# New order of scan pairs, folded MLP norm and later token loads in a Mamba, expert and attention kernel

## The chip, the cores and the metric

One core of one Trainium2 chip. The metric is the device time of the kernel in microseconds, the median of three runs. Five engines work side by side and meet at semaphores only: TensorE (PE), VectorE (DVE), ScalarE (ACT), GpSimd (POOL) and SyncE (SP), which issues the DMAs.

## What is computed

Four layers, each added to its input after a layer norm, on `x` of shape (4, 1024, 256): a selective scan, a mixture of 8 experts of which each token takes 2, a causal linear attention with an MLP, and the same experts once more.

```python
# scan (32 states per channel, 1024 steps in order)
s = jnp.clip(s * A + b_t[:, None, :] * x_t[:, :, None], -10.0, 10.0)
y = jnp.sum(c_t[:, None, :] * s, axis=-1)
...
# experts
h = jnp.maximum(jnp.einsum('nd,edh->neh', xf, w1) + b1, 0.0)
eo = jnp.einsum('neh,ehd->ned', h, w2) + b2
out = jnp.einsum('ne,ned->nd', comb, eo)
...
# attention layer, second half
y = layer_norm(x, ln2_scale, ln2_bias)
y = jax.nn.gelu(y @ w1 + b1) @ w2 + b2
return x + y
```

## The kernel before

`front_part` makes the operands of the scan (normed input, projections, convolution) for the whole sequence and leaves them in DRAM; it ends at about 155 us. `main_part` cuts the sequence into 16 chunks of 64 time steps (of 4 batches: 256 tokens, two tiles of 128). Each engine runs a program of its own, written out by hand as `step(i, c, late)` and turned 14 times in a loop, with single steps ahead and behind. One step holds three chunks at three stages: the scan of chunk `i`; output projection, first experts and attention of chunk `c = i - 1`; MLP and second experts of chunk `late = i - 2`. I call one such step a pass.

The scan is serial. Two time steps are a pair, 32 pairs to a chunk. For pair n, PE makes the inputs (`scan_inputs`, L972, products of B and x rows), DVE makes the new states: in `scan_pair`, each of two steps and two halves has a product with the decay (L1389) and a sum with limits (L1399). Every second pair PE reads the states out (`scan_output`, L988). In PE's program `scan(1)` issues the input of pair n + 1 and, at even n from 2 on, the output of the two pairs before; the input of pair n + 1 waits (`stepped`) until DVE has done pair n - 1. In DVE's program `scan(1)` does pair n. Where `scan` stands in the two programs is the order of the work: pairs lie between the pieces of the other two chunks, to fill gaps on both engines.

The other pieces, on PE: `first_layer` (L1054, three products of high and low parts) and `second_layer` (L1067) of an expert, with the suffix `late_` for the late chunk; `gate` (L1024), `turn_comb` (L1031, transposes the tokens' weights for the experts), `bias` (L1038), transposes (`tpose_set`, L1009), `features`, `scores` (L1148), `from_states` (L1158), `from_chunk` (L1168), `new_states` (L1179), `mlp_input`, `mlp_first`, `mlp_second`. The output projection of attention is L1332. On DVE: `ln_stats`, `ln_apply` (L1428, subtract and scale), `ln_affine` (L1435 and L1440, the same with weight and bias, two instructions a tile for one), `routing` (L1447 to L1459, picks two of eight), `set_acc` (L1475), `add_expert` (L1486), `feature`, `mask` (L1503). ACT copies, and makes relu and gelu between the layers. POOL makes the reciprocal roots of the norms (L799, L801), the low parts (L808) and some additions (L822, L838, L842).

At the start of the main part ACT makes high parts of `f_w1` and `m_w1` (L862) and POOL their low parts, while DVE begins the scan.

SP's `chunk_loads` asks for the tokens of chunk `i` (12 DMAs, L720 to L722) and then for x rows (8 DMAs per four units, L704) and B rows (4 DMAs per unit, L713); a unit is two pairs. Rows are asked for four units ahead, as soon as PE has made the inputs of the unit whose place they take. Ahead of the tokens SP waits in `tokens_free` until the chunk before has used its own:

```python
with looped(sp, 2, CHUNKS - 1) as i:
    tokens_free(i - 1)
    chunk_loads(i, True)
    finish(i - 2)
```

## Time and profile before

| | |
|---|---|
| median of 3 runs | 2336.93 us (2328.58 to 2338.21) |
| profiled execution, its own time | 2337.66 us |
| its span, first to last instruction | 2335.9 us |
| PE busy | 2029.0 us, 87% |
| DVE busy | 1696.1 us, 73% |
| ACT busy | 517.3 us, 22% |
| POOL busy | 259.5 us, 11% |
| mean granted clock of TensorE | 0.923 |

Busy is the time in which an engine runs an instruction; waits for semaphores are not in it. The granted clock is the share of 2.4 GHz that TensorE was given; it knows two levels, 1.0 and 0.5 (1.2 GHz). A row `A <- B: x, n, y` of the view of waits says that A's engine sat idle x us in n times, the longest y, until B had ended. PE instructions of the source appear as two in the trace where they are full float32 products (L1067: 4 in the program, 8 in the trace). The scan runs from 170.7 to 2175.7 us, the first chunk alone, and behind the last there are two more steps without scan.

### The profile page before, as it was taken

Reading aid. Unit: us, or ns where it says so; the run is one execution under the profiler, and the core shown is the slowest. Engines: PE = TensorE matmul, PEld = TensorE weight load, DVE = VectorE, ACT = ScalarE, POOL = GpSimd, SP = SyncE. Lnnn points to the kernel's source line nnn. Section 1 sums busy time; section 2 is a strip of 40 time slices with the busy share of each in tenths; the row PEclk is TensorE's granted clock in tenths of the full one; section 3 lists DMA queues with packets and bytes.
Section 4 is the critical chain, followed back from the end, with each engine's and each line's share of the span. In section 5 each row is a group of like instructions: output and inputs, shape, how many; then the busy total and the mean of one; then the engine's idle time right before and its main releaser. Section 6 shows DMA issues by size and latency. Waiting matters only on the chain. (4 is left out here: it accounts for less than half of the span.)

```text
span 2335.9 us, 58987 instructions
## 1 busy us (share of the span) xinstructions
PE 2029.0 (87%) x18400; PEld 1656.8 (71%) x18400; DVE 1696.1 (73%) x6417; ACT 517.3 (22%) x1078; POOL 259.5 (11%) x337
## 2 busy tenths in 40 slices
PE   7845888989898989989898989889898989899897
PEld 4422666768777777777787778778687777778786
DVE  4539768787787878787876877786786868787542
ACT  3430112121222222121222222221212222221221
POOL 0021001010101110010101111110101011010110
PEclk9875779999999999999998999998998989999998
DMA  7731100000000101010100001010000001010000
GB/s 254 229 109 34 25 12 25 12 25 12 23 18 12 28 9 30 12 30 12 25 12 17 24 12 25 12 30 12 25 12 23 18 12 25 12 30 8 6 1 10
DMA packets 100872, 73.51 MB, mean 31 GB/s; under 512 B 64488, under 2 KB 94448, under 8 KB 99568
## 3 DMA queue, kind: packets, MB, share of 16 engines
q1 hardware_dynamic: 100592, 69.91, 10.7%
q8 instruction: 160, 2.62, 0.5%
q14 instruction: 120, 0.98, 0.1%
HBM read 46.26 MB, written 23.59 MB: 30 GB/s over the span
## 5 line engine op out<-in xcount | busy, mean ns | idle before, releaser
L1389 DVE TENSOR_TENSOR decayed_state<-state,decay 128x128 f32<-128x128 f32 x2048 | 552.0, 311 | 9.9 <-issue 8.0
L1399 DVE CUSTOM_DVE_ANT_0 state<-decayed_state,bank 128x128 f32<-128x128 f32 x2048 | 504.7, 286 | 46.5 <-PE bank L972 19.1
L1067 PE MATMUL bank<-f_w_sb,hs_whole 128*128 128x256 f32 x2048 | 526.2, 402 | 0.6 <-ACT hs_whole L877 0.6
L1067 PEld LDWEIGHTS bank<-f_w_sb,hs_whole 128*128 128x128 f32 x2048 | 390.2, 200 | 87.6 <-ACT hs_whole L877 31.2
L877 ACT ACTIVATE hs_whole<-bank,f_b_sb 128x256 f32<-128x256 f32 x512 | 215.1, 471 | 947.4 <-PE bank L1054 947.4
L972 PE MATMUL bank<-xrows,brows 128*128 128x256 f32 x1024 | 258.2, 345 | 94.9 <-DVE state L1399 56.0
L972 PEld LDWEIGHTS bank<-xrows,brows 128*128 128x128 f32 x1024 | 179.7, 211 | 140.5 <-issue 74.4
L1486 DVE SCALAR_TENSOR_TENSOR x<-bank,comb,x 128x256 f32<-128x256 f32 x256 | 111.9, 478 | 147.9 <-PE bank L1067 147.3
L1486 DVE SCALAR_TENSOR_TENSOR res<-bank,comb,res 128x256 f32<-128x256 f32 x256 | 112.1, 480 | 138.2 <-PE bank L1067 136.6
L988 PE MATMUL bank<-state,cblk 128*32 128x256 f32 x2048 | 178.3, 423 | 35.0 <-DVE state L1399 35.0
L799 POOL TENSOR_TENSOR m_ve<-m_mv,m_eps 128x2 f32<-128x2 f32 x96 | 19.3, 201 | 1580.1 <-DVE m_mv L1423 1580.1
L1054 PE MATMUL bank<-late_fT_parts,f_w_hi 128*128 128x256 f32 x1024 | 187.3, 307 | 0.0
L1054 PE MATMUL bank<-fT_parts,f_w_hi 128*128 128x256 f32 x1024 | 172.9, 294 | 0.0
L1054 PEld LDWEIGHTS bank<-late_fT_parts,f_w_hi 128*128 128x128 f32 x1024 | 149.3, 195 | 12.1 <-issue 6.4
L1054 PEld LDWEIGHTS bank<-fT_parts,f_w_hi 128*128 128x128 f32 x1024 | 141.6, 193 | 6.7 <-issue 5.3
L1067 PE MATMUL bank<-m_w_sb,hs_whole 128*128 128x256 f32 x512 | 120.7, 379 | 0.0
L893 ACT ACTIVATE hs_whole<-bank,m_b_sb 128x256 f32<-128x256 f32 x128 | 53.8, 471 | 225.4 <-PE bank L1054 225.4
L1067 PEld LDWEIGHTS bank<-m_w_sb,hs_whole 128*128 128x128 f32 x512 | 92.4, 189 | 10.1
L988 PEld LDWEIGHTS bank<-state,cblk 128*32 128x32 f32 x2048 | 42.0, 113 | 74.5 <-DVE state L1399 39.3
L1054 PE MATMUL bank<-late_fT_parts,m_w_hi 128*128 128x256 f32 x512 | 90.7, 301 | 2.0 <-issue 2.0
L1054 PEld LDWEIGHTS bank<-late_fT_parts,m_w_hi 128*128 128x128 f32 x512 | 74.0, 199 | 17.5 <-issue 16.3
L1054 PE MATMUL bank<-late_fT_parts,f_w_lo 128*128 128x256 f32 x512 | 83.4, 286 | 0.0
(148 smaller groups left out, 2561.5 us busy)
## 6 DMA issues: line engine op xcount, KB each, us to landing
xrows<-xs_dram SPq DMA_DIRECT2D x512, 32.0 KB
brows<-bs_dram SPq DMA_DIRECT2D x1024, 2.0 KB
xt<-in_x SPq DMA_DIRECT2D x4, 1024.0 KB, 7.9
xn_dram<-xn SPq DMA_DIRECT2D x4, 1024.0 KB, 5.4
z_dram<-zT SPq DMA_DIRECT2D x4, 1024.0 KB, 4.1
f_w_sb<-in_f_w SPq DMA_DIRECT2D x2, 2048.0 KB
xs_dram<-xhi SPq DMA_DIRECT2D x4, 1024.0 KB, 5.2
xs_dram<-xlo SPq DMA_DIRECT2D x4, 1024.0 KB, 8.4
```

Of the source, the lines that this page charges most:

```text
L799: pool.tensor_tensor(ve[:, k], mv[:, k, :, 1], eps[:, k], ALU.add).then_inc(ve_done[k].sem, 1)
L877: act.activation(hs_whole[:, e % 2, m], hidden_bank(c, f, e)[:, m * TOK:(m + 1) * TOK], ACT.Relu, bias=g["f_b1"][:, e, m:m + 1]).then_inc( ...
L893: act.activation(hs_whole[:, j % 2, m], HB[j % 2][:, m * TOK:(m + 1) * TOK], ACT.Gelu_apprx_tanh, bias=g["m_b1"][:, 2 * j + m:2 * j + m + ...
L972: last = pe.matmul(U[n % 2][:, j * D:(j + 1) * D], brows[:, q * USTEPS + tq].rearrange("r b n -> r (b n)"), xrows[:, half % 2, tq, :], sta ...
L988: last = pe.matmul(Y[YCOLS * j:YCOLS * (j + 1), tile * D:(tile + 1) * D], cblk[:, slot * YCOLS:(slot + 1) * YCOLS], state[:, s % RING, :], ...
L1054: last = pe.matmul(dst(tile), *((w_, d_) if stationary == "w" else (d_, w_)), start=first and stationary != "more", stop=(n == len(PRODUCT ...
L1067: last = pe.matmul(bank_[:, tile * D:(tile + 1) * D], hs_whole[:, slot, m, tile * P:(tile + 1) * P], w(m), start=(m == 0 and tile == 0 and ...
L1389: dve.tensor_tensor(decayed_state[:, part], state[:, (s - 1) % RING, part], decay[:, part], ALU.mult).then_inc(decayed.sem, 1)
L1399: dve._custom_dve(add_sat, out=state[:, s % RING, part], in0=decayed_state[:, part], in1=U[n % 2][:, s % 2 * D + h * HALF:s % 2 * D + (h + ...
L1486: dve.scalar_tensor_tensor(out=dst[:, tile], in0=out_bank(c, f, e)[:, tile * D:(tile + 1) * D], scalar=comb[:, f, tile, e:e + 1], in1=dst[ ...
```

## The change

**Scan pairs.** Both programs get new places for `scan`. In the loop over the first experts a table `PAIRS_AT` gives the number of pairs ahead of each expert: none at 0, two at 1, 6 and 7, one at the others. Ahead of the loop stands one pair less, and some places in attention lose their pair, others move. **Order on PE.** `second_layer(c, 0, 0)` goes ahead of `turn_comb`, with a wait for `x3_done`, since the accumulator bank of expert 0 still holds the MLP output. `late_second(5)` goes ahead of `from_states`, `late_first(6)` ahead of `from_chunk(1)`. On DVE the norm for the late experts and the four masks are drawn together.

**Folded norm.** The norm ahead of the MLP loses weight and bias (`ln_apply` for `ln_affine`). At the start, ACT scales the rows of `m_w1` with `ln2_s`, PE multiplies `ln2_b` with the unscaled `m_w1`, and DVE adds that to `m_b1`. The high and low parts are made behind it.

**Tokens.** SP asks for the tokens of a chunk behind the rows of its first five units, `tokens_free` with them.

```diff
-            def chunk_loads(i, more):
-                load_tokens(sp, i)
+            def chunk_loads(i, more, earlier=True):
                 for u in range(UNITS_U if more else UNITS_U - GROUPS_U):
+                    if u == TOKENS_AT:
+                        if earlier:
+                            tokens_free(i - 1)
+                        load_tokens(sp, i)
...
+            act.wait_ge(mlp_bias_made.sem, 1)
+            for k in range(KD):
+                act.activation(g["m_w1"][:, k, :], g["m_w1"][:, k, :], ACT.Copy, scale=g["ln2_s"][:, k:k + 1]).then_inc(mlp_scaled.sem, 1)
+            act.wait_ge(mlp_scaled.sem, KD)
+            act.wait_ge(mlp_bias_set.sem, 1)
...
+            for m in range(MLP // P):
+                for k in range(KD):
+                    last = pe.matmul(TB[:, 2 * m:2 * m + 2], g["m_w1"][:, k, m * P:(m + 1) * P],
+                                     g["ln2_b"][:, k:k + 1].broadcast_to([P, 2]), start=(k == 0), stop=(k == KD - 1))
+            last.then_inc(mlp_bias_made.sem, 1)
...
+        PAIRS_AT = (0, 2, 1, 1, 1, 1, 2, 2)
...
                     tpose_set(c, T_FFN1, xf_done[0])
-                scan(1)
                 mlp_second(3)
                 scan(1)
...
                     first_layer(c, 0, 1)
-                scan(2)
+                scan(1)
+                if c is not None:
+                    if late is not None:
+                        pe.wait_ge(x3_done.sem, x3_done.after(late, 1))
+                    second_layer(c, 0, 0)
+                scan(1)
                 if c is not None:
                     turn_comb(c, 0)
...
                         if e:
-                            scan(1)
+                            scan(PAIRS_AT[e])
...
-                        second_layer(c, 0, e)
+                        if e:
+                            second_layer(c, 0, e)
                         if e == 0:
                             bias(c, 0)
-                            scan(1)
...
                 late_first(3)
-                scan(1)
                 late_second(2)
...
                 features(g["wk"], 0, k_made)
-                scan(1)
...
                 pe.wait_ge(kT_done.sem, kT_done.after(c, 1))
+                scan(1)
                 features(g["wq"], 0, q_made)
...
                 scan(1)
+                late_second(5)
                 pe.wait_ge(masked.sem, masked.after(c, 3))
...
                 from_chunk(0)
-                late_second(5)
-                scan(1)
+                scan(1)
+                late_first(6)
                 from_chunk(1).then_inc(num_made.sem, 1)
                 new_states(0).then_inc(kv_half.sem, 1)
-                late_first(6)
                 scan(1)
...
                 tpose_set(c, T_WO, at_done, HB[1])
-                scan(1)
                 late_second(6)
```

And DVE's program:

```diff
-                scan(3)
+                scan(1)
                 if late is not None:
...
                     ln_stats(late, FFN2, x3, x3_done, (1, 1))
+                scan(1)
                 if c is not None:
                     routing(c, 0)
-                scan(2)
+                scan(1)
+                if late is not None:
+                    ln_apply(late, FFN2, x3, late_turn, xf_done[1])
                 if c is not None:
                     set_acc(c, 0, res, res)
                 for e in range(E):
                     if e:
-                        scan(1)
+                        scan(PAIRS_AT[e])
...
-                ln_affine(LN2, a_t, "ln2_s", lambda tile: rows["ln2_b"][:], late_turn, yl_done)
+                ln_apply(c, LN2, a_t, late_turn, yl_done)
```

The pair between late additions 1 and 2, that between masks 1 and 2 and that ahead of late addition 6 are gone from DVE; one goes behind the key features and one behind late addition 5. The pairs left over come behind the last late addition, three on PE before and four now.

Three places of PE's program in the loop's body show the moves. The listings carry the line numbers of their own kernel: L972, L988, L1031, L1038, L1054 and L1067 of the one are L990, L1006, L1049, L1056, L1072 and L1085 of the other. `REGISTER_ALU` and `ISA` hold waits and counters.

Entry to the first experts, behind the first layers of experts 0 and 1, before:

```order
L972 MATMUL bank<-xrows,brows 128x256 x2
L969 REGISTER_ALU
L972 MATMUL bank<-xrows,brows 128x256 x2
L982 REGISTER_ALU
L988 MATMUL bank<-state,cblk 32x256 x4
L1031 MATMUL bank<-ident_sb,comb 8x128 x2
L1085 ISA
L1067 MATMUL bank<-f_w_sb,hs_whole 128x256 x4
L1038 MATMUL bank<-f_b_sb,combT 128x256 x2
L969 REGISTER_ALU
L972 MATMUL bank<-xrows,brows 128x256 x2
```

The same place now:

```order
L990 MATMUL bank<-xrows,brows 128x256 x2
L1006 MATMUL bank<-state,cblk 32x256 x4
L1103 ISA
L1085 MATMUL bank<-f_w_sb,hs_whole 128x256 x4
L987 REGISTER_ALU
L990 MATMUL bank<-xrows,brows 128x256 x2
L1049 MATMUL bank<-ident_sb,comb 8x128 x2
L1056 MATMUL bank<-f_b_sb,combT 128x256 x2
```

The second layer has moved ahead of the transposes of `comb`, and the bias product follows these at once.

From the second layer of expert 6 to the first late first layer, before:

```order
L1067 MATMUL bank<-f_w_sb,hs_whole 128x256 x4
L969 REGISTER_ALU
L972 MATMUL bank<-xrows,brows 128x256 x2
L982 REGISTER_ALU
L988 MATMUL bank<-state,cblk 32x256 x4
L1054 MATMUL bank<-late_fT_parts,f_w_hi 128x256 x4
```

and now:

```order
L1085 MATMUL bank<-f_w_sb,hs_whole 128x256 x4
L987 REGISTER_ALU
L990 MATMUL bank<-xrows,brows 128x256 x2
L1000 REGISTER_ALU
L1006 MATMUL bank<-state,cblk 32x256 x4
L982 REGISTER_ALU
L984 REGISTER_ALU
L987 REGISTER_ALU
L990 MATMUL bank<-xrows,brows 128x256 x2
L1072 MATMUL bank<-late_fT_parts,f_w_hi 128x256 x4
```

A second input stands directly behind the first.

Ahead of `from_states` (the 64x68 products), behind late first layer 5, before:

```order
L972 MATMUL bank<-xrows,brows 128x256 x2
L988 MATMUL bank<-state,cblk 32x256 x4
L1313 REGISTER_ALU
L1314 REGISTER_ALU
L1158 MATMUL bank<-kv,qT 64x68 x16
L1168 MATMUL bank<-vv,ss 64x17 x32
L1085 REGISTER_ALU
L1067 MATMUL bank<-f_w_sb,hs_whole 128x256 x4
```

and now:

```order
L990 MATMUL bank<-xrows,brows 128x256 x2
L1006 MATMUL bank<-state,cblk 32x256 x4
L1143 REGISTER_ALU
L1103 REGISTER_ALU
L1085 MATMUL bank<-f_w_sb,hs_whole 128x256 x4
L1335 REGISTER_ALU
L1176 MATMUL bank<-kv,qT 64x68 x16
L1186 MATMUL bank<-vv,ss 64x17 x32
```

Late second layer 5 has moved from behind the first `from_chunk` to ahead of `from_states`.

## Rows read from the trace of the kernel before

**Rows 1.** Windows, three passes: length; PE, PEld, DVE, ACT, POOL busy; PEclk; DMA.
```profile
1135.93:1269.30 133.37, 121.58 (x1127) 102.44 (x1127) 100.32 (x390) 28.55 (x61) 14.46 (x19) 0.92 0.07 17
1269.30:1396.21 126.91, 114.38 (x1126) 96.20 (x1125) 100.30 (x390) 28.53 (x61) 14.45 (x19) 0.97 0.08 19
1396.21:1524.98 128.77, 115.19 (x1125) 96.74 (x1124) 100.83 (x390) 28.54 (x61) 14.48 (x19) 0.97 0.08 20
```

**Rows 2.** Who PE waited for, 365 to 2178 us; last line: 2178 to 2336.
```profile
PE bank L1009 <- DVE late_turn L1440: 50.0, 14, 3.6
PE bank L988 <- DVE state L1399: 30.4, 14, 3.0
PE bank L1158 <- DVE ss L1503: 23.5, 14, 1.7
PE bank L972 <- DVE state L1399: 20.3, 14, 1.5
PE bank L1031 <- DVE comb L1459: 18.0, 14, 1.3
PE bank L972 <- DMA brows<-bs_dram: 16.4, 13, 1.5
PE bank L1148 <- ACT ktok L886: 8.8, 14, 0.6
...
PE bank L1038 <- ACT combT L882: 0.5, 1, 0.5
```

**Rows 3.** Three short stretches (columns as in rows 1; PEclk is the granted clock).
```profile
1233.00:1247.00 14.00, 14.00 (x196) 12.23 (x194) 3.69 (x15) 0.84 (x2) 0.00 (x0) 0.51 0.02 4
1366.00:1380.00 14.00, 14.00 (x292) 12.59 (x289) 7.57 (x28) 1.44 (x3) 0.00 (x0) 1.00 0.03 6
1424.00:1428.00 4.00, 4.00 (x24) 2.88 (x24) 2.44 (x11) 0.84 (x2) 0.00 (x0) 0.57 0.03 6
```

**Rows 4.** Timeline around the last experts: start, us, engine, line, operation.
```profile
1322.02 0.58 PE L972 MATMUL bank<-xrows,brows 128*128 128x256 f32 x2
1322.54 0.64 PE L988 MATMUL bank<-state,cblk 128*32 128x256 f32 x8
1323.11 0.74 PE L1054 MATMUL bank<-late_fT_parts,f_w_hi 128*128 128x256 f32 x4
...
1324.61 1.89 PE L1067 MATMUL bank<-f_w_sb,hs_whole 128*128 128x256 f32 x8
...
1322.50 0.88 DVE L1486 SCALAR_TENSOR_TENSOR res<-bank,comb,res 128x256 f32<-128x256 f32 x2 [1.21 <-PE bank L1067]
```

**Rows 5.** Timeline around the MLP norm, DVE and POOL.
```profile
1380.96 0.49 DVE L1389 TENSOR_TENSOR decayed_state<-state,decay 128x128 f32<-128x128 f32 x2
...
1382.08 1.34 POOL L842 TENSOR_TENSOR mb<-mb,a_t 128x512 f32<-128x512 f32 x1
...
1382.63 1.46 DVE L1435 SCALAR_TENSOR_TENSOR late_turn<-a_t,m_mv,ln_s_sb 128x256 f32<-128x256 f32 x2
...
1384.02 0.87 DVE L1440 SCALAR_TENSOR_TENSOR late_turn<-late_turn,m_rstd,ln_b_sb 128x256 f32<-128x256 f32 x2
```

**Rows 6.** Timeline of SP, the first of 12 token loads and what follows the last.
```profile
375.95 0.56 SPq L720 DMA_DIRECT2D x_t<-in_x  x1
...
384.47 3.27 SPq L704 DMA_DIRECT2D xrows<-xs_dram  x8
```

**Rows 7.** Timeline at the start of the main part.
```profile
166.88 1.89 ACT L862 ACTIVATE m_w_hi<-m_w_sb 128x2048 fp32r<-128x2048 f32 x1
167.15 8.83 POOL L808 TENSOR_TENSOR f_w_lo<-f_w_sb,f_w_hi 128x4096 fp32r<-128x4096 f32 x1 [4.52 <-ACT f_w_hi L862]
...
170.74 0.49 DVE L1399 CUSTOM_DVE_ANT_0 state<-decayed_state,bank 128x128 f32<-128x128 f32 x2 [5.90 <-PE bank L972]
171.15 9.48 DVE L1389 TENSOR_TENSOR decayed_state<-state,decay 128x128 f32<-128x128 f32 x2
175.93 4.55 POOL L808 TENSOR_TENSOR m_w_lo<-m_w_sb,m_w_hi 128x2048 fp32r<-128x2048 f32 x1
```

More of the change, by code:

```diff
@@ L118, in build @@
         feature_eps = weight("feature_eps", [P, 1])
-        back = [("a_log", a_log), ("own_batch", own_batch), ("out_w", out_w), *rows.items(),
+        back = [("a_log", a_log), ("own_batch", own_batch), ("out_w", out_w), *rows.items(), ("ln2_s", ln2_s), ("ln2_b", ln2_b),
                 ("gate_w", gate_w), ("gate_b", gate_b), ("before", before), ("f_w1", f_w1), ("f_b1", f_b1),
@@ L1570, in step @@
                 add_late(1)
-                scan(1)
                 add_late(2)
@@ L1586, in step @@
                 mask(1, False)
-                scan(1)
                 mask(2, False)
@@ L1591, in step @@
                 add_late(5)
+                scan(1)
                 dve.wait_ge(num_made.sem, num_made.after(c, 1))
```

27 lines of the change are left out of this document (15 added, 12 removed).

## The prediction, made before the changed kernel was run

> **What bounds the kernel now.** I read four views, in this order. First the span cut into passes. In the steady part a pass is one turn of the loop `step(i, i - 1, i - 2)`, 14 of them between 365.5 and 2178.0 us. They come in three lengths [rows 1]: five of about 127 us, five of about 129 and four of about 133.3; the row shown for each length stands for the others. PE (TensorE) is busy for some 115 us of a 127 us pass, DVE (VectorE) for 100. So PE is the engine to fill, and DVE, with 27 us to spare, matters where PE waits for it.
>
> Second, who PE waits for, over the same 14 passes [rows 2]. The seven rows add up to 167.4 us, 11.96 a pass: 3.57 before the transposes of the MLP input (L1009), 2.17 before scan outputs, nearly all at the end of a pass, 1.68 before `from_states` (L1158), 1.45 before one scan input (L972), 1.29 before the transposes of the expert weights of the tokens (L1031), 1.17 before a scan input whose B rows had not landed, 0.63 before `scores` (L1148). Nearly all of them are PE waiting for DVE, so it is the order of the two programs that costs, not their amount of work.
>
> Third, the granted clock [rows 3]. After `from_states` one pass has level 0.51 (1.2 GHz) over 14 us, and another has 1.00 (2.4 GHz) at the same place: that is the 133 us pass against the 127 us one, 6.4 us. Before the fall PE had sat 1.67 us for the masks and then run the small products. Even the shortest pass has 0.97 [rows 1], so it falls somewhere in each. The 129 us passes differ from the 127 ones by a short fall about 28 us into the pass (0.57 over 4 us, third row of rows 3), behind the L1031 wait, the bias and the wait for rows: 1.9 us each. Over the shortest pass the four long ones cost 25.6 us and the five middle ones 9.5, together 35.
>
> Fourth, the timeline, for unit prices [rows 4, 5]. A scan input takes 0.5 us of PE behind a second layer and 0.3 elsewhere, an output 0.6, a first layer 1.5. On DVE one expert's addition takes 0.8 to 0.9 (0.88 with its end), and a pair of scan steps 1.67 (1380.96 to 1382.63). PE can do the input of pair n+1 only when DVE has done pair n-1, and this ties the two.
>
> **The change, part by part, for one full pass.**
>
> *Token loads behind five units.* SP issued 12 loads of tokens ahead of the rows (375.95 to 384.47, 8.5 us [rows 6]). Now the rows for pair 8 are asked for as soon as pair 1 has its inputs. The wait of 1.17 goes to 0. What is late next: the rows of the tenth unit, now behind the tokens. They are asked for after pair 10, and needed by pair 18, in between lie some 30 us of expert work against about 15 us of issues. I charge nothing.
>
> *Second layer of expert 0 ahead of the transposes.* Its 1.7 us of PE work cover the routing on DVE; 1.29 goes to 0. But now the bias product comes directly behind the transposes and needs ScalarE's copy. The last pass has the two back to back already, and there the wait is 0.5 (the last line of [rows 2]). Net -0.8.
>
> *Two pairs at expert 1, none at 0.* At pair 7 PE needs pair 6 from DVE, which stands behind the accumulator (about 0.8, like an addition) and expert 0: 0.1 + 0.8 + 0.8 + 1.67 = 3.4 us after the bias. PE has a first layer and pair 6 for this time, 1.5 + 0.9. New wait 1.0.
>
> *Two pairs at experts 6 and 7.* At 6 the same sum with the late bias leaves 0.3. At 7, PE's pair 15 needs pair 14, which DVE begins only after adding expert 6: 0.1 + 0.8 + 1.67 = 2.55 after the second layer, while PE has pair 14 alone, 0.85. New wait 1.7. Formerly the late first layer stood behind a single pair here, and no wait.
>
> *Pairs taken from the first half of attention.* Between the late layers 3 and 2 no pair stands any more, and the input after the attention transposes finds its pair done long ago: 1.45 goes to 0. `scores` keeps 0.5 of 0.63, as it still needs late expert 4 and the K copy.
>
> *Late second layer 5 ahead of `from_states`.* 1.7 us of PE work lie over the last two masks: 1.68 goes to 0.1. ScalarE's relu is ready in time, since a pair stands between the two layers. DVE's wait for `num_made` grows, but there it has room.
>
> *Folded MLP norm.* DVE's two products that apply the bias (1384.02 to 1384.89) go: 0.9. Pair 27, which is now last ahead of the transposes, has no output, so PE arrives 0.6 sooner. 3.57 becomes 3.2. The other two products took 1.46 instead of about 0.9 because GpSimd's addition (1382.08, 1.34 us) ran beside them [rows 5], and I let the new `tensor_scalar` suffer the same 0.6; ends 0 and 1.3. The Trainium skill, "SBUF — State Buffer", section "Who interferes with whom", says that such a DVE instruction, if GpSimd came first, is blocked fully until the other ends. By that rule it would end about 0.2 later, and the sum would be 3 us longer.
>
> *One more pair behind the MLP input* (four, were three). From the end of late second layer 7: 0.1 + 0.8 + three pairs (5.0) + 0.1 = 6.0 until the last output may start; PE has 3.5 of work there. 2.17 becomes 2.5.
>
> Sum of waits after: 0.5 + 1.0 + 0.3 + 1.7 + 0 + 0.5 + 0.1 + 3.2 + 2.5 = 9.8, against 11.96: **-2.1 a pass, -29 us over 14.** Each of the three new waits could be nothing, if DVE runs ahead, or one pair (1.67) longer, so a pass lies between -5 and +1.
>
> *The clock.* The long falls came behind 1.67 us of wait and then the small products. The wait goes, but 3 us of small products stay, and `from_chunk(1)`, both calls of `new_states` and the transposes now stand together. The new 1.0 and 1.7 us waits are as large as those behind which the short falls came. I take a quarter of the 35 back: **-8**; ends -35 and +35.
>
> *Start.* 16 small products of `ln2_b` with `m_w1` come ahead of the first scan input, which comes so late that DVE waits 5.9 us for it [rows 7]: hidden. But ScalarE scales `m_w1` (as many elements as take it 1.89 us [rows 7]) and waits for those products first, about 6 us in all, before it makes the high parts. GpSimd's two low parts (8.83 and 4.55 us) move by as much, and it is their end that frees DVE: two scan products took 9.48 us beside them [rows 7]. DVE gets one pair (1.7) done before they begin. The stall of the fifth unit's rows in the first chunk (about 2.8 us) goes, and one of about 2 comes behind the tokens, as SP is full there. **+4**, between 0 and +7.
>
> *First pass with a late chunk missing* (242.8 to 365.5): the same moves at a lower clock, with 29 us of PE waits: -1, between -4 and +3. *The last two passes*: no scan, the fold and the masks: **-1**.
>
> Total: -29 - 8 + 4 - 1 - 1 = -35. The profiled execution took 2337.7 us (its span 2335.9), the median of the runs is 2336.9, so either base gives the same: **2303 us**.
>
> **Rivals.** What separates change from no change in a measurement of this kernel is about 0.5%, 12 us.
>
> *A: the clock gains more than the waits.* If filling the waits keeps the level up in all passes, all 35 us come back: 2303 - 27 = 2276. For it: both kinds of falls lay directly behind waits that go. Against: new waits of the same size. "TensorE: Matmul & The Clock Gate", section "Loop structure matters more than you think", of the Trainium skill, says that matmuls kept back to back stay at the high clock and that waits between them lose it; by that rule this rival holds, if one overlooks the new waits.
>
> *B: the double pairs take it all.* If each of the three doubled places, and the tail, costs PE half to one pair more than I worked out, 2.1 a pass comes back and the time is about 2332. For it: scan steps in a row are DVE's longest work, and PE has only an input between them. Against: the sums above.
>
> *C: slower, by falls of the clock.* If the denser block of small products behind late first layer 6, or the wait of 1.7 at expert 7, brings the 14 us fall in nearly every pass instead of four, ten more passes cost 6.4 each: 2311 + 64 = 2375. It decides from about six more passes on. For it: PE stayed at the low level through just these products [rows 3]. Against: after them now come late second layer 6, the output projection and late first layer 7, which are dense, so that the level should rise sooner.
>
> *D: tokens in the way.* If the rows behind the tokens land late in each pass, 1.2 to 2 us come back per pass: 2320 to 2331. The issues take half of the time that there is, so this is unlikely.
>
> **How the numbers follow.** Forecast 0.46 (2288 to 2325), A 0.22, B 0.15, C 0.10, D 0.07. Faster by over 0.5% are the forecast, A, and a part of B and D: 0.75. Within 0.5% the rest of B and D: 0.15. Slower C: 0.10. The range goes down to the clock gain in full with 1 us a pass more (2265) and up through B to no change (2338).
>
> **What would show it.** Right: no PE wait at L1158, none for B rows in the full passes; waits of PE near 9.8 a pass, with new ones of about 1 and 1.7 among the scan inputs of the expert loop; the MLP wait near 3.2; the first scan step of chunk 1 about 4 us later. Wrong: waits over 12 a pass (B), or more than four passes at granted clock 0.92 or below (C), or none (A).

## The result and the profile after

| | before | changed |
|---|---|---|
| median of 18 runs each, in turns | 2327.34 us (2319.49 to 2345.17) | 2354.76 us (2336.19 to 2363.58) |
| profiled execution, its own time | 2337.66 us | 2353.65 us |
| its span | 2335.9 us | 2351.8 us |
| PE, DVE busy | 2029.0, 1696.1 us | 2049.6, 1688.1 us |
| mean granted clock | 0.923 | 0.918 |

The ratio is 1.0104, with a 95% interval of 1.0082 to 1.0127: slower by 1.0%, 27 us. The forecast was 2303. It started from 2337, the median of three runs; over 18 runs the kernel before has 2327, and the profiled execution of before is 10 us above that, so the two traces lie closer together (15.9 us) than the two medians.

I cut the span at the first scan step of chunks 0, 1 and 2, at the end of the last scan step, and at the end. The two profiled spans differ by 15.9 us: start of the scan +2.8 (170.74 to 173.55), chunk 0 +4.8, chunk 1 -4.6, the 14 full passes +11.2 (1810.0 to 1821.2), tail +1.7. So most of the loss is in the passes, where I had forecast a gain of 37. Three of them, with the columns of [rows 1], and short stretches behind expert 7 in two of them:

```profile
1017.56:1150.73 133.17, 118.84 (x1125) 99.11 (x1124) 100.11 (x388) 28.37 (x61) 14.42 (x19) 0.94 0.08 20
1282.47:1413.20 130.73, 116.63 (x1125) 97.78 (x1124) 99.61 (x388) 28.38 (x61) 14.36 (x19) 0.96 0.08 21
1805.67:1932.90 127.23, 116.20 (x1126) 97.45 (x1125) 99.58 (x389) 28.30 (x61) 14.37 (x19) 0.96 0.08 19
1073.00:1078.00 5.00, 4.70 (x21) 4.22 (x22) 2.06 (x11) 0.84 (x2) 0.00 (x0) 0.66 0.03 5
1338.00:1342.00 4.00, 3.56 (x23) 3.36 (x24) 2.20 (x11) 0.84 (x2) 0.00 (x0) 1.00 0.03 6
```

The shortest pass is 126.8 us, as long as the shortest of before, the longest 133.5. Who PE waited for, 368.5 to 2189.8 us (to be laid beside [rows 2]):

```profile
PE bank L990 <- DVE state L1422: 67.7, 42, 2.7
PE bank L1027 <- DVE late_turn L1451: 54.8, 14, 3.9
PE bank L1072 <- issue: 12.4, 12, 1.5
PE bank L990 <- issue: 12.0, 5, 3.1
PE bank L1166 <- ACT ktok L899: 8.9, 14, 0.7
PE bank L1056 <- ACT combT L895: 6.5, 14, 0.5
PE bank L1006 <- DVE state L1422: 0.7, 1, 0.7
PE bank L1219 <- DVE z_t L1537: 0.5, 1, 0.5
```

The waits for DVE's masks (L1158 of before), its weights of the tokens (L1031) and the B rows are gone, as forecast. In the passes PE waited 163.5 us in all, 10.5 less than before (174.0, with short ones that [rows 2] leaves out), not 29. Two things eat the rest: 24.4 us called "issue", for which before has 3.5, and the MLP wait, which went up from 50.0 to 54.8 where it should have gone down by 5. One of the "issue" waits, PE at the head of a pass (start, us, operation, and in brackets the idle time before it):

```profile
1282.27 0.63 PE L1072 MATMUL bank<-late_fT_parts,m_w_hi 128*128 128x256 f32 x4
1282.74 0.39 PE L1072 MATMUL bank<-late_fT_parts,m_w_lo 128*128 128x256 f32 x2
1284.60 0.51 PE L1072 MATMUL bank<-late_fT_parts,m_w_lo 128*128 128x256 f32 x2 [1.47 <-issue]
```

It stands in the middle of a product of one layer; nothing that PE could wait for in data lies there. The profile's list of DMA queues has a hint. Instructions come to the core through queues of their own; first the row of before, then that of the changed kernel (packets, MB, share):

```profile
q8 instruction: 160, 2.62, 0.5%
```

```profile
q8 instruction: 172, 2.82, 0.5%
```

These packets have 16 KB. Sorted by time, before has ten in nearly every pass, the changed kernel eleven. The trace shows some 2,370 instructions of PE in a pass, 237 for each of ten packets. I take the queue to be PE's; the runs with a shift, below, bear that out.

And the clock: 197 us of the passes ran at half clock, 167 before. It fell at about 57 us of a pass in nine of the fourteen passes, where before it never did: that is the stretch 1073 to 1078 above, behind expert 7. The wait there stands in every pass, so in five of them it had no fall behind it; 1338 to 1342 is one of these.

### The profile page after: what moved, and what is told of

The parts are those of the page before. It is cut to its first block and busy times, and to the rows that moved or that the text cites. A ratio compares the mean times of both kernels' runs of the same rounds, so it can differ in the third digit from the quotient of the medians.

```text
span 2351.8 us, 59011 instructions
## 1 busy us (share of the span) xinstructions
PE 2049.6 (87%) x18432; PEld 1669.7 (71%) x18432; DVE 1688.1 (72%) x6386; ACT 518.1 (22%) x1080; POOL 258.3 (11%) x337
## 5 line engine op out<-in xcount | busy, mean ns | idle before, releaser
L1412 DVE TENSOR_TENSOR decayed_state<-state,decay 128x128 f32<-128x128 f32 x2048 | 565.1, 317 | 10.4 <-issue 7.8
L1085 PE MATMUL bank<-f_w_sb,hs_whole 128*128 128x256 f32 x2048 | 529.7, 404 | 3.4 <-DVE ss L1526 1.0
L1085 PEld LDWEIGHTS bank<-f_w_sb,hs_whole 128*128 128x128 f32 x2048 | 394.0, 202 | 95.0 <-ACT hs_whole L890 37.8
L990 PE MATMUL bank<-xrows,brows 128*128 128x256 f32 x1024 | 258.8, 342 | 126.0 <-DVE state L1422 107.0
L990 PEld LDWEIGHTS bank<-xrows,brows 128*128 128x128 f32 x1024 | 174.6, 205 | 195.1 <-DVE state L1422 121.5
L1509 DVE SCALAR_TENSOR_TENSOR res<-bank,comb,res 128x256 f32<-128x256 f32 x256 | 112.1, 479 | 126.5 <-PE bank L1085 125.1
L1006 PE MATMUL bank<-state,cblk 128*32 128x256 f32 x2048 | 183.9, 433 | 3.3 <-DVE state L1422 2.4
L1072 PE MATMUL bank<-late_fT_parts,f_w_hi 128*128 128x256 f32 x1024 | 184.3, 304 | 0.0
L1072 PE MATMUL bank<-fT_parts,f_w_hi 128*128 128x256 f32 x1024 | 172.6, 294 | 0.0
L1072 PEld LDWEIGHTS bank<-late_fT_parts,f_w_hi 128*128 128x128 f32 x1024 | 149.4, 195 | 6.0 <-issue 0.7
L1072 PEld LDWEIGHTS bank<-fT_parts,f_w_hi 128*128 128x128 f32 x1024 | 139.5, 191 | 11.6 <-issue 10.3
L1085 PE MATMUL bank<-m_w_sb,hs_whole 128*128 128x256 f32 x512 | 121.7, 381 | 0.0
L1072 PE MATMUL bank<-late_fT_parts,m_w_hi 128*128 128x256 f32 x512 | 101.9, 329 | 0.0
L1085 PEld LDWEIGHTS bank<-m_w_sb,hs_whole 128*128 128x128 f32 x512 | 93.3, 192 | 10.3
L1072 PEld LDWEIGHTS bank<-late_fT_parts,m_w_hi 128*128 128x128 f32 x512 | 84.2, 225 | 15.4 <-issue 14.4
L1027 PE MATMUL bank<-ident_sb,late_turn 128*128 128x128 f32 x128 | 25.0, 330 | 66.7 <-DVE late_turn L1451 66.7
L1072 PE MATMUL bank<-late_fT_parts,f_w_lo 128*128 128x256 f32 x512 | 83.0, 285 | 0.0
```

Source lines behind the costliest of these rows:

```text
L990: last = pe.matmul(U[n % 2][:, j * D:(j + 1) * D], brows[:, q * USTEPS + tq].rearrange("r b n -> r (b n)"), xrows[:, half % 2, tq, :], sta ...
L1006: last = pe.matmul(Y[YCOLS * j:YCOLS * (j + 1), tile * D:(tile + 1) * D], cblk[:, slot * YCOLS:(slot + 1) * YCOLS], state[:, s % RING, :], ...
L1027: last = pe.transpose(dst[:, kk * TOK + tile * P:kk * TOK + (tile + 1) * P], src[:, tile, kk * P:(kk + 1) * P], ident[:])
L1072: last = pe.matmul(dst(tile), *((w_, d_) if stationary == "w" else (d_, w_)), start=first and stationary != "more", stop=(n == len(PRODUCT ...
L1085: last = pe.matmul(bank_[:, tile * D:(tile + 1) * D], hs_whole[:, slot, m, tile * P:(tile + 1) * P], w(m), start=(m == 0 and tile == 0 and ...
L1412: dve.tensor_tensor(decayed_state[:, part], state[:, (s - 1) % RING, part], decay[:, part], ALU.mult).then_inc(decayed.sem, 1)
```

## The experiments

All but one were measured in five rounds (the exception in three), in turns with the kernel before. I give for each run: the 14 passes in its profiled execution, PE's waits in them, the passes less the waits ("work"), and the part at half clock, summed from the trace's record of the granted clock. A profiled execution is one run; the median is of 5 to 18. The four rows of repeats are the same built programs once more (see below) and show how far two executions of one program lie apart: 12 us in the passes and 24 us at half clock between before and e4, 17 at half clock between e1 and e12.

| run | passes | waits | work | half clock | median | ratio, 95% |
|---|---|---|---|---|---|---|
| before | 1810.0 | 174.0 | 1636.0 | 167 | 2327 to 2330 | |
| changed | 1821.2 | 163.5 | 1657.7 | 197 | 2354.76 | 1.0082 to 1.0127 |
| repeat of before (e4) | 1798.4 | 174.7 | 1623.7 | 143 | 2328.96 | 0.9984 to 1.0033 |
| repeat of changed (e6) | 1813.9 | 159.9 | 1654.0 | 187 | 2352.14 | 1.0061 to 1.0156 |
| e1 fold | 1813.9 | 180.9 | 1633.0 | 159 | 2345.71 | 1.0026 to 1.0091 |
| repeat of e1 (e5) | 1809.4 | 178.7 | 1630.7 | 150 | 2342.13 | 1.0033 to 1.0088 |
| repeat of e1 (e12) | 1807.2 | 181.0 | 1626.2 | 142 | 2344.77 | 1.0039 to 1.0091 |
| e2 tokens | 1766.9 | 161.7 | 1605.2 | 95 | 2294.88 | 0.9827 to 0.9901 |
| e3 order | 1812.7 | 168.2 | 1644.5 | 182 | 2347.55 | 1.0061 to 1.0139 |
| e8 tokens, order | 1811.5 | 167.4 | 1644.1 | 171 | 2347.99 | 1.0062 to 1.0114 |
| e7 tokens, fold | 1820.4 | 175.5 | 1644.9 | 200 | 2355.56 | 1.0073 to 1.0143 |
| e13 before, shifted 64 | 1831.1 | 194.0 | 1637.1 | 171 | 2360.70 | 1.0116 to 1.0227 |
| e14 fold, shifted 192 more | 1776.7 | 163.9 | 1612.8 | 113 | 2316.14 | 0.9936 to 0.9988 |
| e15 tokens, fold, 192 | 1767.9 | 148.4 | 1619.5 | 125 | 2318.21 | 0.9928 to 1.0006 |
| e16 changed, 192 | 1790.5 | 153.2 | 1637.3 | 142 | 2343.20 | 1.0046 to 1.0108 |
| e9 both parts of the order | 1797.0 | 161.4 | 1635.6 | 143 | 2338.47 | 1.0022 to 1.0068 |
| e10 expert part | 1772.1 | 158.1 | 1614.0 | 106 | 2304.05 | 0.9868 to 0.9924 |
| e11 tokens, layer 5 early | 1767.2 | 138.0 | 1629.2 | 146 | 2299.20 | 0.9860 to 0.9916 |
| e17 e10 and attention's pairs | 1787.6 | 152.1 | 1635.5 | 164 | 2319.76 | 0.9933 to 0.9981 |
| e18 e10 and attention's layers | 1753.7 | 142.5 | 1611.2 | 81 | 2293.79 | 0.9817 to 0.9886 |

Two readings of the table carry the rest. The work is the same products in every row and yet runs from 1605 to 1658 us; it goes up with the time at half clock, by some 0.4 us for each (30.8 us from e2 to before, at 72 us more of half clock). That is rough: e16, with the new order, and e4 have the same half clock and 13.6 us between their work, and this part was not explained. And the passes are waits plus work: who takes waits away can lose them again as clock.

**The three parts alone.** e1 has the fold alone, all `scan` calls as before. e2 has the tokens alone. e3 has the new places of pairs and layers alone, on both engines, with `ln_affine` as before.

```diff
-                load_tokens(sp, i)
                 for u in range(UNITS_U if more else UNITS_U - GROUPS_U):
+                    if u == TOKENS_AT:
+                        if earlier:
+                            tokens_free(i - 1)
+                        load_tokens(sp, i)
```

> The kernel before with the folded norm alone, old order and old token loads. Theory 1, code placement: the 16 products at the start stand ahead of PE's loop and shift its code; the changed kernel shows waits of PE for no releaser ('issue') of 1.2 us two microseconds into a pass and of 3 us at its head, 24.4 us over 14 passes, which before had 3.5. If the shift makes them, this kernel shows them too: start +6 us (PE's products took 7.0 us where I had 6 and hidden), passes -0.9 each by the shorter chain (-13) and +20 by the waits, together +10 to +18. Theory 2, the order alone is to blame: no such waits here, start +6, chain -13: -12 to -2.

> The kernel before with the token loads behind five units alone. Both theories: the wait for B rows (16.4 us over the full passes) goes, the first chunk is about the same: -10 to -20 us. If the rows were late for another reason: 0. If the freed 1.2 us a pass are given back by the scan input behind them (DVE's state): -3 to 0.

> The kernel before with the new order of both programs alone (scan pairs, second layers, DVE's norm and masks), old norm, old token loads. Theory 2, the new waits of 1.0 and 1.9 us in the expert loop and the falls of the clock behind them (56 to 57 us into the pass in ten passes of the changed kernel) cost more than the removed waits gave: +10 to +25 us. Theory 1: the order gives what it should, -5 to -20 us, if the loop keeps its place; PE's program ahead of the loop has the same length here but for a few waits.

Measured: fold 2345.71, tokens 2294.88, order 2347.55. Only the smallest edit is fast, and it is faster than both kernels. The fold came out as theory 1 had it, the order as theory 2; the tokens gained twice what I expected. e2's waits fell by 12 us, its work by 31 (by 13 and 18 against e4). Before, the clock fell behind the wait for rows in five passes, 28 us into them; here are the same places of a pass in the trace of before and in that of e2, and then the place 97 us into a pass where before had its long falls and one whole pass of e2:

```profile
522.50:527.50 5.00, 5.00 (x29) 3.71 (x28) 2.34 (x11) 0.84 (x2) 0.00 (x0) 0.66 0.03 6
```

```profile
521.00:526.00 5.00, 5.00 (x40) 4.20 (x39) 4.48 (x18) 1.93 (x4) 0.07 (x1) 1.00 0.19 52
1476.00:1490.00 14.00, 12.91 (x263) 11.06 (x261) 9.92 (x39) 3.24 (x8) 1.35 (x3) 1.00 0.02 3
1503.98:1630.27 126.29, 114.44 (x1126) 96.96 (x1126) 100.93 (x390) 28.54 (x61) 14.47 (x19) 0.97 0.08 19
```

Both kinds of falls are gone, in all 14 passes; thirteen of the passes have 126.2 to 126.5 us. The order alone also removes the wait for rows (16.4 to 1.2 us), and those for masks and for the tokens' weights. But its waits in all go down by 6 us only, since the MLP wait grew from 50.0 to 67.9 and two new places stand among the scan inputs, and it has its own falls: half clock 182 us, 151 of them from 108 us of the pass on, where before has 97.

```profile
PE bank L973 <- DVE state L1402: 72.9, 41, 2.8
PE bank L1010 <- DVE late_turn L1443: 67.9, 14, 4.9
```

e3 has 160 packets on q8, as before, and 2 us of "issue": its loss has nothing to do with them. The fold alone takes 14 us off the MLP wait and gets 12.9 of "issue" at the head of the pass in return.

**Empty instructions that were none.** The bias products are 64 more instructions for PE ahead of its loop. I wanted to test whether their place is what matters, with `pe.nop(nofuse=True)` ahead of the main part: 64 in before (e4), 192 in the fold, the changed kernel and tokens with fold (e5, e6, e7), 32 in the fold (e12).

> The kernel before with 64 empty instructions on PE ahead of the main part's first product, where PE waits for rows anyway; nothing else. It shifts the loop's code by what the 16 products take (32 products and 32 weight loads in the trace). Theory 1: waits of PE for no releaser near the head of the pass, as in the changed kernel, and +12 to +25 us. Theory 2: no difference, within 0.3%.

> The kernel before with the folded norm alone, and 192 empty TensorE instructions ahead of the main part. With the bias products' 64 instructions they move TensorE's loop by 256 instructions, as much as one of the 16 KB packets that reach the core ten times in a pass of before and eleven times in a pass of the folded one. Theory (code placement): the folded norm alone lost because its loop then spans an eleventh packet, and TensorE waits for it some 1.4 us a pass (17.8 us counted as issue, at rows of the pass where before has 3). Then this run has ten packets a pass, under 5 us of issue waits and keeps the norm's gain of 1.0 us a pass: 2310 to 2325 us, ratio 0.992 to 0.998. Rival (the fold itself, by the clock's falls or the start): the waits stay, and the time stays at 2340 to 2350, ratio 1.003 to 1.009.

> The changed kernel with the same 192 empty TensorE instructions. Theory (code placement): ten packets a pass instead of eleven, the 24 us of issue waits fall under 5, and the time falls from 2354 by 15 to 25 us, to 2330 to 2340, ratio 1.000 to 1.005. Rival (placement doesn't matter): 2348 to 2360, ratio above 1.008. In either case the clock's falls behind expert 7 stay, so that half clock time in the fourteen passes stays over 170 us.

> Tokens behind five units of rows and the folded norm, no new order, with the 192 empty instructions. If parts add up and placement was the fold's loss: the tokens' 34 us less and the norm's 10 to 15 us less, 2278 to 2290 us, ratio 0.978 to 0.984, with the MLP wait near 2.7 us a pass and no wait for rows. If the fold itself costs: 2300 to 2315. If the tokens' gain was a clock state that any other timing loses: 2315 to 2335.

> Tokens behind five units and the new order, no folded norm (so the full change without the fold). The order alone had lost the wait for rows already, so by the theory that the order's loss is its own (wait at expert 7 and fewer pairs in the attention part, clock falling behind both) the tokens add little here: 2340 to 2352 us, ratio 1.005 to 1.010, half clock time 170 to 190 us. If parts add up instead, the tokens' 34 us come off 2347: 2310 to 2320, ratio 0.992 to 0.996, and the changed kernel's loss would lie with the fold.

> The kernel before with the folded norm and 32 empty TensorE instructions. With 192 of them TensorE's packets kept their places in the pass, as they did with 64 in the kernel before; the packets may start at multiples of 64 instructions, so that only the rest of a division by 64 counts. Theory: with 32 the packets move by up to 32 instructions against the program; ten a pass instead of eleven and no issue waits, 2320 to 2335. Rival: eleven packets and the waits stay, 2340 to 2350, as with 192.

Measured: e4 2328.96 (1.0008), e5 2342.13 (1.0061), e6 2352.14 (1.0108), e12 2344.77 (1.0065). These are the numbers of before, e1 and the changed kernel once more, and for a plain reason: the built programs hold none of the empty instructions (q8 has 160 packets in e4, as in before, and 172 or 173 in the others). So they say nothing on placement, for or against either theory, but they show how well the ratios repeat: the fold has 1.0059, 1.0061, 1.0065. e7 is tokens with fold: 2355.56, and the tokens' 34 us are gone; I had 2278 to 2335 in three cases, and none of them holds. Its loop has the fold's place, with 27.8 us of "issue" and 200 us at half clock. e8 is the order with tokens: 2347.99 against 2347.55 without. The order had freed the wait for rows already, and the tokens bring nothing more, as I had expected (2340 to 2352). Put the other way round, the order on top of the tokens costs 53 us (e2 to e8); of the 45 us by which the passes differ, 39 are work. The parts do not add up.

**Placement, with instructions that stay.** Waits that are already met stay in the program (two in the source make one). They stand where PE idles ahead of the main part, 128 in the source and 64 in the program for e13, 384 and 192 for e14, e15 and e16:

```diff
+            for _ in range(128):
+                pe.wait_ge(pool_set.sem, 1)
             pe.wait_ge(g["back_in"], BACK_IN)
```

> The kernel before with 64 waits that are already met at the head of TensorE's main part, where it idles 17 us: its loop then lies 64 instructions further on, as the folded norm's bias products place it, and nothing else is changed. (The empty instructions of the runs labelled pad had been dropped when those kernels were built, so that they were repeats: of before, of the fold, of the changed kernel and of tokens with fold.) Theory (code placement): eleven 16 KB packets a pass instead of ten, 13 to 25 us of issue waits at the head of the passes, time up by 8 to 20 us: 2336 to 2348, ratio 1.003 to 1.008. Rival (placement does nothing; the waits come from the fold): ten packets, 2325 to 2332.

> The kernel before with the folded norm and 192 waits already met, so that TensorE's loop lies 256 instructions further on than before. Theory: ten packets a pass, issue waits under 5 us, 2310 to 2325 us, ratio 0.992 to 0.999. Rival: eleven packets and 2340 to 2348 again.

> Tokens behind five units and the folded norm, with the 192 waits already met. Without them it took 2356 us, with 28 us of issue waits and 155 us at half clock in the passes. Theory (placement took the fold's gain and set off the clock's falls): ten packets, no issue waits, half clock near the 64 us of the tokens alone, and the norm's 1.0 us a pass: 2278 to 2292 us, ratio 0.979 to 0.985. Rival (the fold itself sets off the falls, by another phase): 2300 to 2345.

> The changed kernel with the 192 waits already met. Theory: ten packets, the 24 us of issue waits gone, the order's own loss left (tokens with the order took 2348), less the norm's gain: 2325 to 2340, ratio 0.999 to 1.005. Rival (placement doesn't matter): 2350 to 2360.

e13 took 2360.70 us: the kernel before, with nothing changed but the place of its loop, is 1.7% slower. Its packets and PE's waits over the passes, against [rows 2]:

```profile
q8 instruction: 172, 2.82, 0.5%
```

```profile
PE bank L1011 <- DVE late_turn L1442: 50.3, 14, 3.6
PE bank L990 <- DVE state L1401: 29.6, 13, 3.1
PE bank L974 <- DMA brows<-bs_dram: 24.6, 13, 2.1
PE bank L1160 <- DVE ss L1505: 23.5, 14, 1.7
...
PE bank L1056 <- issue: 13.6, 13, 1.8
```

The second instruction queue, q14, keeps its 120 packets. The time is above the theory's range (2336 to 2348), the packets and the waits are the theory's. The waits for DVE are as before to 1 us; added are 13.6 us in the MLP's products at the head of the pass, and 8 us at the rows, 20 in all. Start and tail are as before (170.0 and 160.7 us): what is added lies in the passes. Against the profiled execution of before it is 21 us, nearly all of them waits; against e4, whose time is nearer to the median, it is 33 us, 19 of them waits and 13 work, at 28 us more of half clock. And the other way round, e14 (fold, shifted by 64 + 192 = 256 instructions against before, about one packet by the count above) has its ten packets and its waits back:

```profile
q8 instruction: 161, 2.64, 0.5%
```

```profile
PE bank L1006 <- DVE state L1420: 36.6, 13, 2.9
PE bank L1027 <- DVE late_turn L1449: 36.0, 14, 2.6
PE bank L1176 <- DVE ss L1524: 22.1, 14, 1.6
...
PE bank L990 <- issue: 3.6, 13, 0.3
```

Its passes take 37 us less than e1's, its median is 29.6 us lower; the 192 waits cost 11 us at the start (scan from 185.8 us, e1 174.8). So the fold in itself is a gain, and lost by where it put the loop. One control is missing: before with 256 instructions more and no fold was not run. In e16 the changed kernel's passes fall from 1821.2 to 1790.5; the waits called "issue" go from 24.4 to 2.2, of which 12 come back as waits for DVE. Its median falls by 11.6, with 13 us given to the start (186.5 against 173.6), and lies above the 2325 to 2340 of the theory. Without that price it would stand near 2330, level with before; this sum was not run. e15 did not come to 2278 to 2292 as the theory had it. Its passes go up and down in turn:

```profile
1013.08:1141.39 128.31, 116.77 (x1125) 98.62 (x1124) 100.98 (x389) 28.49 (x61) 14.53 (x19) 0.95 0.08 20
1141.39:1265.68 124.29, 114.09 (x1127) 96.47 (x1127) 99.53 (x389) 28.49 (x61) 14.47 (x19) 0.98 0.08 19
```

The shorter kind is 2 us under e2's pass (10.2 us of waits against 11.8); the longer one, with 11.5 us of waits, lies 2 us above it, with a fall at its head and another about 95 us into it. The mean is e2's pass. Its time lies in the rival's range (the clock falls in another phase), and the falls are there: 125 us at half clock against 95. (By the count of the table e2 has 95 us at half clock and e7 has 200, where the expectation has 64 and 155.) Against e7, which is e15 without the 192 waits, it is 37 us faster.

**What in the order loses.** e9: tokens and order, with one pair at expert 7 and the pair between late layers 1 and 2 back. e10: of that order only the expert part. e17 and e18 add to e10 either kind of attention's moves, and e9 has both.

```diff
-        PAIRS_AT = (0, 2, 1, 1, 1, 1, 2, 2)
+        PAIRS_AT = (0, 2, 1, 1, 1, 1, 2, 1)
```

That is in all four. e11 has, on top of e2, this alone (and e18, on top of e10, the same and `late_first(6)` ahead of `from_chunk(1)`):

```diff
                 scan(1)
+                late_second(5)
                 pe.wait_ge(masked.sem, masked.after(c, 3))
...
                 from_chunk(0)
-                late_second(5)
                 scan(1)
```

e17, on top of e10, moves pairs alone (PE's part; DVE's likewise):

```diff
                 features(g["wk"], 0, k_made)
-                scan(1)
...
                 pe.wait_ge(kT_done.sem, kT_done.after(c, 1))
+                scan(1)
...
                 tpose_set(c, T_WO, at_done, HB[1])
-                scan(1)
```

> Tokens behind five units and the new order, but with one pair at expert 7 instead of two, and the pair between the last expert layers 1 and 2 back at its old place. Theory (the double pair at expert 7 costs a wait of 1.9 us, behind which the clock falls at 57 us of a pass): no fall between 50 and 70 us of a pass (tokens and order had 17 us of half clock there, the changed kernel 31), the wait at pair 15 gone, 10 to 20 us less than the 2348 of tokens with the full order: 2328 to 2338. Rival (the loss lies in the attention part, half clock from 108 us of a pass on): 2340 to 2350, and the half clock time there stays at 130 to 150 us.

> Tokens behind five units and the expert part of the new order alone (two pairs at experts 1 and 6, the second layer of expert 0 early), with one pair at expert 7, so that the attention part and the end of the pass are as before. If the order's loss lies in its attention part: near the tokens alone, 2290 to 2305, ratio 0.984 to 0.991, half clock time under 100 us. If it lies in the expert part: 2320 to 2345.

> Tokens behind five units, and the second layer of expert 5 moved ahead of the attention read from the states, where the kernel before waits 1.6 us a pass for the masked scores. Theory (a wait that hides nothing is worth its length, as long as no clock fall is set off): 14 passes less 1.5 us, 2270 to 2280 us, ratio 0.976 to 0.980. Rival (the wait returns at the next operation, since the chain of VectorE sets the pass): 2290 to 2300, the time of the tokens alone. Third: the move sets off falls of the clock as the full order did, 2310 to 2340.

> As e10 (tokens, expert part with one pair at expert 7), and of the attention part the scan pairs' new places alone: the second expert layers 5 and 6 stay where they were. Theory (with the pairs gone from the attention part and more of them at the end of the pass, VectorE's chain of the MLP's norm starts as late as before, and the part around 108 to 124 us, in which TensorE runs the pairs with waits, falls to half clock more often): MLP wait up from 3.6 to 4.5 us or more a pass, half clock in 108 to 124 us of the passes up from 75 to about 115 us, 2325 to 2338 us, ratio 0.999 to 1.004. Rival (the layers' moves cost it): 2300 to 2310.

> As e10, and of the attention part the moves of the last experts' layers alone (second layer of expert 5 ahead of the read from the states, first layer of expert 6 ahead of the second half from the chunk), all scan pairs as in e10. The move of layer 5 alone on top of the tokens took away the 1.6 us wait for the scores in each pass and gave no time, since the clock fell in 13 of 14 passes at 100 to 108 us of the pass. Theory (pairs are the loss): 2300 to 2312 us, ratio 0.988 to 0.993, with such falls. Rival (the layers' moves are the loss): 2325 to 2338.

*The double pair at expert 7.* The changed kernel, around pair 15:

```profile
1205.52 0.88 DVE L1509 SCALAR_TENSOR_TENSOR res<-bank,comb,res 128x256 f32<-128x256 f32 x2 [0.66 <-PE bank L1085]
...
1205.55 0.64 PE L1006 MATMUL bank<-state,cblk 128*32 128x256 f32 x8
...
1208.10 0.50 PE L990 MATMUL bank<-xrows,brows 128*128 128x256 f32 x2 [1.91 <-DVE state L1422]
1208.33 0.54 PEld L1072 LDWEIGHTS bank<-late_fT_parts,f_w_hi 128*128 128x128 f32 x4
```

The addition of expert 6 ends at 1206.4, then come two steps of pair 14; PE waits 1.91 us. This wait is in all 14 passes, and the clock falls right behind it in nine passes of the changed kernel, in five of e8 and four of e3, so the wait by itself does not decide it. In e9, where the wait is gone, there is no fall between 50 and 70 us of any pass; half clock is 171 - 143 = 28 us less than in e8, 17 of them in that stretch, and the median is 9.5 us lower, just above the theory's 2328 to 2338. e9 also puts back the pair between the late layers 1 and 2, and with it a wait of 1.45 us; the two were not tried apart.

*Attention.* e10 (2304.05, 106 us at half clock) has the time that I gave for a loss in the attention part, 9 us over e2. From there the pairs' moves cost 16, the layers' moves gain 10, and both together cost 34. With the pairs gone the MLP wait is 67.9 us instead of 49.9 (e9 and e17 alike), and half clock goes from 106 to 164 us (e17), mostly between 108 and 124 us of the pass. The MLP wait and the half clock are those that e17's theory had, the time (2319.76) lies between its range and the rival's; e18 is under both of its ranges. Neither kind alone explains e9: 29 us come only from the two together.

*Layer 5 alone* (e11) shows how a wait taken away can be worth nothing. Against e2 its waits are 23.7 us lower, as forecast, and its passes are the same to 0.3 us. The time (2299.20) is the rival's, but not for the rival's reason: the wait did not return. What ate it is what the third case has. In all 14 passes the clock falls at about 100 us of the pass, where e2 has no fall:

```profile
1354.00:1358.00 4.00, 4.00 (x83) 2.96 (x84) 1.76 (x9) 0.84 (x2) 0.00 (x0) 0.57 0.00 0
1379.76:1506.02 126.26, 115.91 (x1126) 97.65 (x1126) 100.76 (x391) 28.54 (x61) 14.62 (x19) 0.96 0.08 19
```

PE was busy for the whole of these 4 us, with late first layer 6 above all. For the 6 us before them it was busy too, on small products with one scan input between:

```profile
1347.46 1.17 PE L1159 MATMUL bank<-kv,qT 128*64 128x68 f32 x32
1348.56 2.04 PE L1169 MATMUL bank<-vv,ss 64*64 64x17 f32 x64
1350.53 0.50 PE L973 MATMUL bank<-xrows,brows 128*128 128x256 f32 x2
1350.96 2.04 PE L1169 MATMUL bank<-vv,ss 64*64 64x17 f32 x64
1352.94 0.73 PE L1180 MATMUL bank<-vv,ktok 64*32 64x17 f32 x64
1353.60 0.74 PE L1055 MATMUL bank<-late_fT_parts,f_w_hi 128*128 128x256 f32 x4
```

In e2 late second layer 5 stands in the middle of this block, 2 us of 128x256 products. In e18 layer 5 has moved too, but late first layer 6 stands there in its place, and this fall is there in one pass only. That fits, but nothing was run to test it, and the long falls of before came with layer 5 in the middle. e18 is the fastest kernel of the study: 2293.79 us (2287.09 to 2298.75), 1.5% under before. Against e2 (2294.88) that is no difference that can be told.

## Why the prediction was wrong

**Most waits that I followed by their instructions came out well. Two steps failed: the list of waits had no term for PE's own instructions, and the clock's term had the wrong sign.** For the passes I had -29 and -8, together -37; measured were -10.5 and +21.7, together +11.2. So 18 us of the miss are waits and 30 are clock and work. Step by step, per pass:

- *Token loads*: wait 1.17 to 0, right. What it is worth alone was not: 34 us, not 16 (e2 against before), as the clock's falls behind it went too. In the changed kernel it is worth nothing (e3, e8).
- *Bias behind the transposes* 0.5: measured 6.5 / 14 = 0.46. *Two pairs at expert 1*: 1.0, measured 0.98. *Expert 7*: 1.7, measured 1.91. *Expert 6* 0.3, *attention's input* 0, *`from_states`* 0.1: no wait. *`scores`* 0.5: 0.63. *End of pass* 2.5: 1.6 to 2.1.
- *MLP norm* 3.2 (3.27 by its own terms): measured 3.91. I let GpSimd's addition lengthen the new `tensor_scalar`. It ran beside pair 27 instead:

```profile
1266.66 1.59 DVE L1412 TENSOR_TENSOR decayed_state<-state,decay 128x128 f32<-128x128 f32 x2
1266.84 1.26 POOL L849 TENSOR_TENSOR mb<-mb,a_t 128x512 f32<-128x512 f32 x1
...
1268.69 0.73 DVE L1451 TENSOR_SCALAR late_turn<-a_t,m_mv,m_rstd 128x256 f32<-128x256 f32 x2
```

  Two products of the scan took 1.59 us instead of 0.49, and they stand ahead of the norm as well. The fold took what it should (1.0 in e1); the order put 1.28 on top (67.9 / 14 = 4.85 in e3). It comes with the moved pairs: e17 has it, e10 and e18 don't. That half I had counted as 0.6 only.
- *Sum of waits* 9.8 without the short ones. Without "issue" it is 9.9, so the sum for DVE's and ScalarE's waits was right to 0.1: errors of either sign cancel in it. Over 14 passes the waits should have gone down by 29. **The first step that failed is that this list was complete**: 24.4 us of waits for PE's own instructions came in, 21 more than before. I had costed the 16 bias products at nothing in the passes, since they run once; what they do is to move the loop. e13 shows this without any other part, e16 gives it a size here: some 25 us of the time (11.6 in the median and 13 given to the start).
- *The clock* -8, with ends at -35 and +35: the half clock time went up by 30 us and the work by 21.7. **This is the second step that failed, and the larger one**: I let the falls that would go outweigh those that the new order would bring, and it is the other way round. The order without the fold and with ten packets (e8) is some 20 us over before, with waits down by 7 and work up by 8 (by 20 against e4). Of rival C's two places the wait at expert 7 does it (31 us at half clock, before none), and the falls are short, not of 14 us; from 97 to 108 us the four long falls went and seven shorter ones came, and from 108 us on half clock rose from 97 to 127 us, which no case had. The 35 us were partly luck of the trace, too: e4, the same program, had two long falls and 143 us at half clock, not four and 167. Rival A had all 35 us come back. The Trainium skill, "TensorE: Matmul & The Clock Gate", section "Loop structure matters more than you think", sets matmuls kept back to back against long waits between them; those here are of 0.2 to 4.9 us, and in e11 they fell by 24 us while the time at half clock rose by 51, so fewer waits are no forecast of the clock in this kernel.
- *Start* +4: +2.8 at the start and +4.8 in chunk 0 make 7.6 (chunk 1 begins at 250.4, before at 242.8), just past the end of my range. PE's 16 products took 6.96 us at 1.2 GHz and ended at 172.4 us, where the first scan input had begun at 169.8 before, and the stall of rows behind the tokens was 4.75 us, not 2. *First pass* -1: -4.6. *Tail* -1: +1.7.

Cases: C's sign was right and had 0.10; its price (more passes with long falls) was not what happened. Slower by 1.0% came from two things of like size: the order, some 20 us over before by itself (e3, e8), and the placement, some 25 us (e13, e16); the fold's own gain, some 18 us (e8 to e16, less the 13 of its start), stands against them, and the tokens' gain is lost in the order. What stays open: why the clock falls at a given place in one kernel and not in another could not be worked out from waits and busy time; why the order's two kinds of moves in attention cost so much more together than each alone; and why eleven packets cost PE a wait at the head of the pass was not tried further than by the shift.

## What to carry to other kernels

Where an engine's loop is so long that its code comes in packets at every turn, an edit ahead of the loop is an edit of the loop: count the instruction packets per turn and the waits called "issue" before judging the edit, and measure it at a second placement. Price a removed wait by the time of the passes, not by its length: in this kernel it was worth anything from nothing (e11) to twice its length (e2), as the clock goes. And try the parts of a change alone: here the smallest one held all of the gain (1.4%), and the whole had lost it. Last, take a second execution of the same program before the clock is priced from one trace.

## What the runs showed of the hardware that I had not expected

- 64 instructions more ahead of PE's loop: eleven 16 KB packets a pass instead of ten, 20 us more of PE's waits over 14 passes, 34 us in the median (e13). 192 more on top of the fold's 64 undo it (e14, e16).
- The longest of these waits are 1.5 to 1.8 us, some 2 us into the pass, and in the changed kernel up to 3.1 us at its first scan input.
- The clock fell to 1.2 GHz while PE was busy without a gap (e11, 4.00 of 4 us at 0.57, and busy on small products for 6 us before), and in e15 at the head of every second pass and 96 us into it, while the passes between had neither fall (seven passes of each kind, all of the same program).
- Two executions of one program differ by 24 us at half clock in the passes (before and e4, 167 and 143).
- 192 waits that were already met put the scan 11 to 13 us later, 64 of them none (170.0 against 170.7).
